# Own work lists for every stretch of a two-layer transformer kernel, a re-ordered setup, and three small edits

## The reference, cut to what matters

```python
x = x + _layernorm(_L0_attn_ref(_layernorm(x), ...))  # a convolution of x along time with a decaying complex exponential
x = x + _layernorm(_L0_ffn_ref(_layernorm(x), ...))   # 8 experts, best two by a softmax router, and a shared expert
x = x + _layernorm(_L1_attn_ref(_layernorm(x), ...))  # 16 heads of 64, l2-normed q and k, ALiBi, causal, 2 null keys
x = x + _layernorm(_L1_ffn_ref(_layernorm(x), ...))   # 4 different experts, best two by their logits
```

## Time and profile before

| what | us |
|---|---|
| median of 3 runs | 1247.14 (1246.96 to 1247.65) |
| the profiled execution's own time | 1255.19 |
| its span in the trace | 1253.5 |
| PE busy | 1057.7 (84% of the span) |
| DVE busy | 798.5 (64%) |
| ACT busy | 549.1 (44%) |
| POOL busy | 594.9 (47%) |

### The profile page before, as it was taken

One profiled execution on the slowest core, in us unless ns is written; L12 is line 12 of the kernel. 1 busy time (PEld: TensorE's weight loads), 2 busy tenths in 40 slices (PEclk: granted clock), 3 DMA queues, 4 the chain that ended last, 5 costly groups with the idle time before them and its releaser, 6 DMA issues.

```text
span 1253.5 us, 18844 instructions
## 1 busy us (share of the span) xinstructions
PE 1057.7 (84%) x6847; PEld 858.6 (69%) x6847; DVE 798.5 (64%) x2546; ACT 549.1 (44%) x1035; POOL 594.9 (47%) x522
## 2 busy tenths in 40 slices
PE   0275789898998899898999999889999899898866
PEld 0254578767786678767886778767886688678744
DVE  7765655686648674686648674786648664764244
ACT  1112643375326633374427533374427543483311
POOL 4003734475526644475427544474527542574312
PEclk9977789899998999999999999899998999899978
DMA  7000000000000000000000000000000000000000
GB/s 181 25 1 1 9 1 1 1 1 10 10 1 0 10 9 1 1 1 10 9 1 1 10 9 1 1 10 1 9 1 1 1 10 1 1 1 9 1 1 9
DMA packets 21852, 11.29 MB, mean 9 GB/s; under 512 B 7424, under 2 KB 21120, under 8 KB 21632
## 3 DMA queue, kind: packets, MB, share of 16 engines
q1 hardware_dynamic: 17584, 7.57, 2.4%
q10 hardware_dynamic: 4176, 2.52, 0.7%
HBM read 7.99 MB, written 2.10 MB: 8 GB/s over the span
## 4 chain that ended last, share of the span: by engine, by line
PE 60%; DVE 23%; ACT 6%; issue 6%; POOL 4%; DVEq 0%; POOLq 0%; ACTq 0%
PE bank L1517 9%; PE bank L1308 6%; PE bank L1547 5%; PE bank L1301 4%; PE bank L1519 4%; PE bank L1302 3%; PE bank L1303 3%; PE bank L1481 3%; PE bank L1427 3%; ACT square L756 2%; PE bank L1487 2%; PE bank L1571 2%; DVE sumsq L1148 2%; PE bank L1622 2%; PE bank L1627 2%
## 5 line engine op out<-in xcount | busy, mean ns | idle before, releaser
L627 POOL TENSOR_TENSOR rnorm<-sumsq,minus_half 128x16 f32<-128x16 f32 x64 | 197.3, 3097 | 35.0 <-DVE sumsq L1151 35.0
L635 POOL TENSOR_TENSOR unit<-unit,causal 128x256 f32<-128x256 f32 x128 | 91.6, 746 | 159.2 <-ACT unit L794 158.6
L635 POOL TENSOR_TENSOR square<-square,causal 128x256 f32<-128x256 f32 x128 | 92.0, 750 | 68.6 <-ACT square L794 68.6
L1175 DVE TENSOR_TENSOR denom<-bank,null_sum 128x4 f32<-128x4 f32 x128 | 20.6, 161 | 154.9 <-PE bank L1519 154.5
L1481 PE MATMUL bank<-qT,kT 64*128 64x256 f32 x512 | 102.2, 394 | 0.0
L800 ACT ACTIVATE qT<-bank 128x512 f32<-128x512 f32 x64 | 38.5, 601 | 142.4 <-PE bank L1308 142.4
L1517 PE MATMUL bank<-val,square 128*128 128x128 f32 x512 | 83.2, 285 | 12.7 <-DVE mixed L1179 11.8
L1517 PE MATMUL bank<-val,unit 128*128 128x128 f32 x512 | 81.9, 282 | 8.5 <-DVE mixed L1179 4.5
L749 ACT ACTIVATE unit<-bank 128x512 f32<-128x512 f32 x128 | 71.9, 599 | 38.4 <-PE bank L1303 35.7
L1487 PE MATMUL bank<-qT,kT 64*128 64x128 f32 x512 | 85.9, 289 | 0.7 <-ACT val L773 0.7
L1308 PEld LDWEIGHTS bank<-ident,unit 128*128 128x128 f32 x520 | 61.4, 147 | 34.3 <-issue 23.3
(11 more groups left out here) (368 smaller groups left out, 2817.3 us busy)
## 6 DMA issues: line engine op xcount, KB each, us to landing
xin<-in_L_attn_x SPq DMA_DIRECT2D x8, 256.0 KB, 2.9
out<-x SPq DMA_DIRECT2D x8, 256.0 KB, 2.3
square<-in_L_attn_w_kv ACTq DMA_DIRECT2D x1, 1024.0 KB, 5.4
unit<-in_L_attn_w_q SPq DMA_DIRECT2D x1, 512.0 KB, 5.3
w_out<-in_L_attn_w_out SPq DMA_DIRECT2D x1, 512.0 KB, 5.3
w_sw<-in_L_ffn_sw_w ACTq DMA_DIRECT2D x2, 256.0 KB, 7.8
unit<-in_L_ffn_experts_gate SPq DMA_DIRECT2D x1, 256.0 KB, 3.4
unit<-in_L_ffn_experts_up SPq DMA_DIRECT2D x1, 256.0 KB, 3.8
```

Of the source, the lines that this page charges most:

```text
L627: pool.tensor_tensor(rnorm[:, k, t, :], sumsq[:, t % 2, k, :], minus_half[:], ALU.pow).then_inc(a_root.sem, 1)
L635: m = pool.tensor_tensor(pd, pd, causal[:].unsqueeze(1).to_broadcast([P, 2, P]), ALU.mult)
```

## The change

One list per engine becomes six: `PROLOGUE` (new order), `FIRST`, `MIDDLE`, `LAST_L`, `LAST_A`, `LAST_F`, each with its own order. The other edits are:

- Setup: POOL makes only the time row, the identity and `minus_half` before the first norm; the rest is in steps `s_sel`, `s_slopes`, `s_fill`, `s_colb`. `val` is no longer filled whole (only its column of ones and its tail). ACT issues the first `x` and the layer-0 weights; SP issues everything else in one row. Rounding to the `hi` part, the halving of `w_down` and `w_sw2`, the scalings by gamma and the biases of `s_alibi` move from DVE to ACT; the `lo` parts stay on DVE. The eight copies of `s_pad` are one.
- `l_x` turns tile 0 into bank 4 and the others into bank 5. ACT and DVE make tile 0's two parts first, and `a_m.0` waits for these alone; `a_m.1` waits for the rest.
- `f_route` on PE is gone: `w_cr` holds the context weights and the router's side by side, 136 columns, and one set of four matmuls fills banks 6 and 7. DVE adds the biases of both results in two operations each instead of one, and `f_me.0`, which writes bank 7, waits for both.
- In the last attention (group 7) odd heads use bank 4, so a head waits for the head before the last.

```diff
+MIDDLE = {
+    "PE": """
+a_m.0 a_m.1 a_null f_turn f_ce f_sw.0 f_me.0 l_turn2 a_t.0 f_ceT f_sw.1 a_m.2 f_sw.2 f_relu.0 a_v.0 f_relu.1 a_t.1
...
+            play(steps, table(FIRST[name]), e=2, l=1, a=0)
             for i in range(1, G - 2):
-                play(steps, order(name, 1, 1, 1, 1), e=i + 2, l=i + 1, a=i, f=i - 1)
+                play(steps, table(MIDDLE[name]), e=i + 2, l=i + 1, a=i, f=i - 1)
...
+        def pv_bank(g, h):
+            return 4 if g == G - 1 and h % 2 else 3
...
+        def ce_and_logits(b):
+            return bank[6 + b][:, 0:2 * (P + 8)].rearrange("p (t d) -> p t d", t=2)
...
+            act.dma_start(xin[:], xv[0]).then_inc(x0_loaded, 16)
...
+            def s_w0():
+                act.wait_ge(loaded1, 16 * 7)
+                for w, full in ((w0_router, w0_router_raw), (w0_gate, w0_gate_raw), (w0_up, w0_up_raw)):
+                    act.activation(w.hi, full, ACT.Copy).then_inc(w0_rounded, 1)
+                act.activation(w0_down[:], w0_down[:], ACT.Copy, scale=0.5).then_inc(w0_rest, 1)
...
+            def s_scale():
+                act.wait_ge(loaded2, 16 * LOADS2)
+                act.activation(w_q_raw, w_q_raw, ACT.Copy, scale=col["gamma"]).then_inc(wq_scaled, 1)
+                act.activation(w_kv.hi, w_kv_raw, ACT.Copy, scale=col["gamma"]).then_inc(qkv_rounded, 1)
...
-                act.activation(xaT.hi, bank[5][:], ACT.Copy).then_inc(l_xc.sem, 1)
+                act.activation(xaT.hi[:, 0:P], bank[4][:, 0:P], ACT.Copy).then_inc(l_xc.sem, 1)
+                act.activation(xaT.hi[:, P:], bank[5][:, P:], ACT.Copy).then_inc(l_xc.sem, 1)
...
+                dve.wait_ge(l_xc.sem, l_xc.at(g, 1))
+                low(xaT[:, 0:P], bank[4][:, 0:P])
                 dve.wait_ge(l_xc.sem, l_xc.at(g))
-                low(xaT, bank[5][:])
+                low(xaT[:, P:], bank[5][:, P:])
...
-                V.tensor_tensor(ce_rows[:], rows3(bank[6][:]), row_ce[:].unsqueeze(1).to_broadcast([P, T, D]), ALU.add).then_inc(f_ced.sem, 1)
+                for b in range(2):
+                    V.tensor_tensor(ce_rows[:, 2 * b:2 * b + 2, :], ce_and_logits(b)[:, :, 0:P], row_ce[:].unsqueeze(1).to_broadcast([P, 2, D]), ALU.add).then_inc(f_ced.sem, 1)
...
-                    if t == 0 and k == 0:
-                        pe.wait_ge(l_low.sem, l_low.at(g))
+                    if t < 2 and k == 0:
+                        pe.wait_ge(l_low.sem, l_low.at(g, 3 + t))
...
+                if pv_bank(g, h) == 4 and h == 1:
+                    pe.wait_ge(f_eb.sem, f_eb.at(g - 1, E1))
+                elif known(g) and g == G - 1 and h:
+                    pe.wait_ge(a_mix.sem, a_mix.at(g, 3 * (h - 1)))
+                elif h:
                     pe.wait_ge(a_mix.sem, a_mix.at(g, 3 * h))
...
-            def f_route(g):
-                pe.wait_ge(f_cols.sem, f_cols.at(g))
-                for t in range(T):
-                    last = mm(bank[7][:, 8 * t:8 * t + 8], xmT[:, t * P:(t + 1) * P], w1_router[:], start=True, stop=True)
-                last.then_inc(f_routed.sem, 1)
...
-                    last = mm(bank[6][:, t * P:(t + 1) * P], xmT[:, t * P:(t + 1) * P], w_ce[:], start=True, stop=True)
+                    last = mm(ce_and_logits(t // 2)[:, t % 2, :], xmT[:, t * P:(t + 1) * P], w_cr[:], start=True, stop=True)
...
-                    pe.wait_ge(f_pick.sem, f_pick.at(g, 1))
+                    pe.wait_ge(f_pick.sem, f_pick.at(g, 2))
+                    pe.wait_ge(f_ced.sem, f_ced.at(g, 2))
```

518 lines of the change are left out of this document (335 added, 183 removed).

## The result

The changed kernel takes 1170.05 us in the median of its runs (1168.89 to 1174.75), the kernel before 1247.39 in the same sessions. The ratio is 0.936, with a 95% interval of 0.932 to 0.939: faster by 77 us, where I had forecast 60. The profiled execution has a span of 1169.2 us and a time of 1170.98, so here it stands 0.9 above the median, while that of before stood 8.05 above. Between the two profiled executions the step is 84.2 us; the sum that it has to be laid beside is −59.7.

The account below looks back on a forecast made before the run. DVE's in-order list was taken to bound the prologue, PE with about ten gaps a MIDDLE stage. Terms −22.0 − 4 − 24 − 2 − 6.5 − 1.2 = −59.7 from 1255.2 give 1195.5, less 8.05 about 1187 us; range 1172 to 1210.

Parts of the forecast that it names:

- Prologue: Setup up to a_m.0, bound by DVE's in-order list: a_m.0 from 113.92 to 91.9 us, −22.0 (range −13 to −25).
- the tables: Phase tables in the setup: DVE's 2.92 us wait for POOL goes and POOL's constants get shorter, −4.5 us.
- e_sum: Setup checkpoint on DVE: weight operations ahead of it go, POOL's two gains then bound it, ready at 22 us, −10.
- FIRST: First stretch after the setup: PE's 6.88 us norm wait falls to 5, smaller gaps give 2, −4 us (0 to −10).
- MIDDLE, first half: Stage start −0.4 us (PE's wait for xaT_lo), router and context −1.5 us, per MIDDLE stage.
- the router's 1.8 us: PE time saved per MIDDLE stage by merging the router's matmul set, 1.88 us at a low clock, into the context's.
- MIDDLE, second half: Per stage: 2.01 us wait for l_hg.0 and the clock dip behind it go, less new gaps and late heads, −2.9 us.
- `f_me.0`'s new wait: In MIDDLE, PE's f_me.0 now waits for both DVE bias operations: estimated slack 0.5 us, no cost; uncovered, 1 us.
- the slower rival: PE idles at f_me.0, clock falls to 1.2 GHz, some 8 us a stage lost: 1255 us, chance 0.03.
- LAST_L: Stretch like MIDDLE without group i+2: start, router and first half gain as there, no second-half gap, −2.0 us (0 to −3).
- LAST_A: Last attention: first half −1.5, second bank removes most of 5.8 us in seven head waits, −5.0; −6.5 (−3 to −8).
- the clock stays up: Rival: shorter gaps keep 2.4 GHz, FIRST gets 6 us more, MIDDLE 1.5 each: 1174 us, chance 0.12.

Follow-up runs that it names:

- b_second_new: Kernel before, with the five full MIDDLE stages in the new order behind the first scores on all engines: 1228.3 us, ratio 0.982.
- b_hg0_early: Kernel before, with DVE's step l_hg.0 moved ahead of f_out.3 and the first head in all stretches: 1251.92 us, ratio 1.001.

## Why the prediction was wrong, point by point

- **Prologue** (−22.0 forecast, −19.8): right in mechanism and in its size within 10%. The terms that were off are the tables (−4.5 for a wait that ACT's exponential took over in part, and three operations that POOL's constants hold up by 1.1 us) and `e_sum` (POOL's gains hold DVE up). From `l_res` to `l_down` 9.3 us were won, where I had 8.2. From there to `a_m.0` it takes 17.3 us, for which my sum had 18.2. These two hid half of the loss in front, which was luck.
- **FIRST** (−4, −9.6): the wait came out as forecast, 4.34 us where I had 5, and idle time fell by 3.9 us, which is my −4. The step that failed is the clock behind the wait: I let it stay slow for 13 us as in the earlier trace rows, and it was 0.89 in the 15 us behind the wait, against 0.57 with the old order. I had this case as the end of the range (−10).
- **MIDDLE, first half** (−1.9, about −1.3 by the work done): near. But the router's 1.8 us were no part of it, as undoing them cost a stage nothing.
- **MIDDLE, second half** (−2.9, −6.3): the failed step, with 17 of the 24.5 us by which the sum missed the profiled step (3.4 in each of five stages). I priced the wait that the trace names, 2.0 us and the slow clock behind it, and booked its removal to one step's move. Neither the mechanism nor the size stood. The move alone takes the slow clock away and leaves the stage as long as it was (140.1). With the old order in the changed kernel the wait is 0.83 us, the clock doesn't fall behind it, and the stage is 4.3 us longer. The order of the whole half gives 4.7 us a stage in the old kernel and 6.3 by the work done in the new one: 3.1 of idle time and 3.2 of busy time, of which about 1.5 is the clock. Which of its moves does it stays open.
- **`f_me.0`'s new wait**: I said no cost with 0.5 us of slack. It waits 0.76 us here, and 3.8 us on four occasions in the whole run (the longest 1.89, in LAST_L). The stages are shorter all the same. Behind three of the four the granted clock is 1.00 for the next five us. Behind the longest it fell, as the slower rival had it, but once in the run and by 0.34 of five us (1.7 us). So that rival had its fall once, and not its size:

```profile
886.00:891.00 5.00, 5.00 (x20) 3.67 (x21) 3.62 (x15) 2.81 (x6) 3.43 (x2) 0.66 0.00 0
```

- **LAST_L** (−2, −4.3): I took "the gap wasn't there" as nothing to win; it has the same kind of second half. With the old list it is 134.7, so the order gave 3.6 to 3.8.
- **LAST_A** (−6.5, −11.3): the bank gave 7.3 where I had 5.0. The rest is 1.5 for the other small edits and 2.5 for the list, where I had 1.5 together.
- **LAST_F** (−1.2, −1.7): right, though by edits and not by its list: 56.1 with the old list, 55.8 with its own.
- **From profiled execution to median**: I took 8.05 off because the profiled execution of before stood so much above. The one of after stands 0.9 above. This error of 7 us hid part of the other: the sum missed by 24.5, the median by 17.
- **The range** had −7 as the end of a MIDDLE stage, and −7.5 was measured; the range as a whole took no case in which several terms were at that end at once. The rival "the clock stays up" (1174) comes nearest to the result in number. It is right for FIRST, where it had 6 us more. For MIDDLE it isn't the cause: the clock gave about 1.5 us a stage in the second half, which my sum had already, and in the first half it still fell in several stages.

## What to carry to other kernels

A wait that a trace shows at a step can be a debt of the engine that ends it, and then moving that one step moves the debt (2.01 us became 2.00 at the next head). So price a new order by all that its stretch could give back, and not by the wait of the step that moved: the half stage held 5.8 us of idle time and about 1.5 of slow clock, and the new order gained 6.3. Waits removed in a row of matmuls give back more than their idle time, 7.3 us for 5.7 here. Try a new order as a whole, too: each of my three small moves in the old kernel gave nothing or cost time, and the whole half gave 4.7 us a stage.

## What was not expected of the hardware

- At a granted clock of 1.00 in both, the same 467 PE instructions count 55.35 us busy with the seven waits for the head before among them and 53.69 without these.
- The clock's fall at a stage's start comes and goes between executions of one kernel (0.68 in one, 1.00 in another, for the five us of the context projection) and between the stages of one execution (0.50 to 1.00). A stage with it is 0.6 to 0.9 us longer in the changed kernel and 2.5 in `b_second_new`.
- A DVE operation of 0.35 us takes 1.29 beside a POOL multiplication, and ends 0.15 us behind it.
- With one step moved (`b_hg0_early`) the slow clock behind a 2.0 us wait went from 0.75 to 1.00, the wait stayed, and the stage took as long as before.
- The prologue of one kernel takes 94.1 in one execution and 90.8 in another, with the same instructions.
